# Causal mask and row maxima of the second attention: product on TensorE and reduction, or one fused pass on VectorE

## The reference

```python
def _L1_attn_ref(x, W_qkv, W_o):          # x: 8 x 256 x 128, 16 heads of 8 features
    q, k, v = split(x @ W_qkv)
    q, k = _rope(q, k)
    att = einsum('bhtd,bhsd->bhts', q, k) / sqrt(8)
    att = att + triu(full((256, 256), -inf), 1)
    w = softmax(att, axis=-1)
    y = einsum('bhts,bhsd->bhtd', w, v)
    return concat_heads(y) @ W_o
```

## Time and profile before

| | us |
|---|---|
| runs: median (lowest to highest) of 3 | 635.62 (633.32 to 635.85) |
| the profiled execution's own time | 635.56 |
| its span, first to last instruction | 633.7 |
| TensorE busy | 576.3 (91%) |
| VectorE busy | 404.8 (64%) |
| ScalarE busy | 266.4 (42%) |
| GpSimd busy | 226.7 (36%) |
| mean granted TensorE clock | 0.955 of full speed |

### The profile page before, as it was taken

How to read it: one execution, slowest core, us unless ns; L and a number is a source line. 1 busy time by engine, 2 the same in 40 slices (tenths; PEclk the granted TensorE clock), 3 DMA queues, 4 the chain that set the end, 5 groups by cost and what they waited for, 6 DMA issues and landing times.

```text
span 633.7 us, 11896 instructions
## 1 busy us (share of the span) xinstructions
PE 576.3 (91%) x4428; PEld 447.1 (71%) x4428; DVE 404.8 (64%) x1057; ACT 266.4 (42%) x531; POOL 226.7 (36%) x327
## 2 busy tenths in 40 slices
PE   3899999999987799999789999999889999999994
PEld 3657667766756599899556666665558888888883
DVE  2477877787764733554657788877246666666655
ACT  3586755575630322220055555555632222222220
POOL 2264545554320535363735555554510000000000
PEclk9699999999978999999959999999869999999999
DMA  5953131223000600002221221220000000000000
GB/s 208 324 197 122 69 134 67 102 100 125 10 1 0 252 1 1 1 2 68 70 74 49 63 63 48 68 73 4 4 1 0 2 1 18 1 18 2 1 18 17
DMA packets 25352, 37.64 MB, mean 59 GB/s; under 512 B 3536, under 2 KB 15568, under 8 KB 24912
## 3 DMA queue, kind: packets, MB, share of 16 engines
q1 hardware_dynamic: 25296, 36.89, 17.5%
HBM read 10.01 MB, written 1.05 MB: 17 GB/s over the span
## 4 chain that ended last, share of the span: by engine, by line
PE 63%; DVE 18%; issue 8%; ACT 3%; POOL 3%; DMA 2%; SPq 2%; POOLq 0%; DVEq 0%; ACTq 0%
PE f_O L1611 7%; PE f_O L801 6%; PE f_H L59 5%; PE f_H L61 5%; PE f_H L60 5%; PE a_MI L485 5%; DVE a_UA L366 4%; PE a_S L1328 4%; PE a_Y L437 4%; PE a_YP L1357 3%; PE a_S L1336 3%; PE a_PJ L59 2%; DVE a_m L1172 2%; PE a_S L423 2%; DVE a_rr L357 2%
## 5 line engine op out<-in xcount | busy, mean ns | idle before, releaser
L226 POOL TENSOR_TENSOR a_Y<-a_Y 128x256 f32<-128x256 f32 x64 | 59.5, 933 | 97.0 <-ACT a_Y L265 97.0
L366 DVE SCALAR_TENSOR_TENSOR a_UA<-a_UA,a_mask 128x768 f32<-128x768 f32 x64 | 68.3, 1075 | 27.1 <-ACT a_UA L273 26.6
L1172 DVE TENSOR_REDUCE a_m<-a_S 128x3 f32<-128x384 f32 x117 | 63.7, 554 | 31.6 <-PE a_S L1336 26.5
L1479 ACT ACTIVATE f_sg<-f_H 128x512 f32<-128x512 f32 x64 | 38.2, 597 | 103.1 <-PE f_H L61 103.1
L1557 DVE TENSOR_TENSOR f_hid<-f_H,f_sg 128x512 f32<-128x512 f32 x64 | 44.3, 692 | 53.2 <-PE f_H L61 43.1
L273 ACT ACTIVATE a_UA<-a_S,a_one 128x768 f32<-128x768 f32 x64 | 57.6, 900 | 44.8 <-PE a_S L424 44.6
L1096 POOL TENSOR_SCALAR_AFFINE_SELECT f_w<-f_w 128x256 f32<-128x256 f32 x128 | 51.8, 407 | 67.9 <-ACT f_w L1143 67.7
L1143 ACT ACTIVATE f_w<-a_ST 128x384 f32<-128x384 f32 x118 | 56.9, 493 | 39.7 <-PE a_ST L1334 39.7
L1611 PEld LDWEIGHTS f_O<-f_w,f_hid 128*128 128x128 f32 x512 | 65.9, 191 | 8.1 <-issue 3.3
L1611 PE MATMUL f_O<-f_w,f_hid 128*128 128x128 f32 x512 | 67.8, 276 | 2.0 <-DVE f_acc L1535 2.0
L437 PE MATMUL a_Y<-a_UA,a_V 128*64 128x256 f32 (+1 forms) x512 | 58.4, 351 | 0.0
(11 more groups left out here) (282 smaller groups left out, 1390.0 us busy)
## 6 DMA issues: line engine op xcount, KB each, us to landing
a_q<-a_c_h SPq DMA_DIRECT2D x16, 256.0 KB, 2.5
a_q<-a_c_l SPq DMA_DIRECT2D x16, 256.0 KB, 2.6
a_k<-a_c_h SPq DMA_DIRECT2D x16, 256.0 KB, 2.5
a_k<-a_c_l SPq DMA_DIRECT2D x16, 256.0 KB, 2.6
f_w<-in_f_w SPq DMA_DIRECT2D x1, 2048.0 KB, 8.8
a_q<-a_c_h SPq DMA_DIRECT2D x16, 128.0 KB
a_q<-a_c_l SPq DMA_DIRECT2D x16, 128.0 KB
a_k<-a_c_h SPq DMA_DIRECT2D x16, 128.0 KB
```

The source lines that it names most:

```text
L226: pool.tensor_tensor(Y2[:, v % 2, j, :], Y[:, v % 2, j, :], Y[:, v % 2, j, :], ALU.mult).then_inc(y2_ready, 1)
L366: dve.scalar_tensor_tensor(UA[:, j % 4, :, :], UA[:, j % 4, :, :], 1.0, mask[:, None, :].to_broadcast([P, 2, SW]), ALU.add, ALU.mult).then ...
L1172: dve.tensor_reduce(m3[:, b % 2, h % H1, :], s_bank(h)[:, 0:SW].rearrange("p (a n) -> p a n", a=3), AX.X, ALU.max).then_inc(max_done, 1)
```

## The change

The mask product is gone from both places, and the S products are each complete by themselves (`stop=True`). `s_ready` is now raised by the second S product. On VectorE each head has two fused passes in place of the reduction: one over the 256 columns of the second half of the queries, one over the 128 of the first. Each adds the mask to the scores, writes the sum as bf16 to `masked` (four buffers, which nothing reads) and writes the maximum over its columns to one column of `row_max`. `mask_b` keeps its size, but its first 128 columns are now zeros: the pass over 256 columns reads all of it, the pass over 128 its second half. `row_max` has the layout that mm had, so L1176, L1177 and `mm_ready` go, and in place of the wait for `mm_ready` a batch waits for `mx_ready` of the batch two before it.

```diff
-        m3 = sb("m3", [P, 2, H1, 3])
-        mm = sb("mm", [P, 2, H1])
+        row_max = sb("row_max", [P, 2, 2, H1])
+        masked = sb("masked", [P, 4, SW], BF16)
...
                     if b >= 2 and h % H1 == 0:
-                        dve.wait_ge(mm_ready, 2 * (b - 1))
-                    dve.tensor_reduce(m3[:, b % 2, h % H1, :], s_bank(h)[:, 0:SW].rearrange("p (a n) -> p a n", a=3), AX.X, ALU.max).then_inc(max_done, 1)
+                        dve.wait_ge(mx_ready, b - 1)
+                    for t, cols in ((1, slice(0, L)), (0, slice(L, SW))):
+                        width = P + t * P
+                        i = dve.tensor_tensor_reduce(out=masked[:, h % 4, cols], in0=s_bank(h)[:, cols], in1=mem["mask_b"][:, L - width:L], scale=1.0, scalar=-3e38,
+                                                     op0=ALU.add, op1=ALU.max, accum_out=row_max[:, b % 2, t, h % H1:h % H1 + 1])
+                    i.then_inc(max_done, 1)
                 if maxima_at(g, MAX - 2) is not None:
                     b = maxima_at(g, MAX - 2)
                     dve.wait_ge(max_done, (b + 1) * H1)
-                    dve.tensor_tensor(mm[:, 1, :], m3[:, b % 2, :, 0], m3[:, b % 2, :, 1], ALU.max).then_inc(mm_ready, 1)
-                    dve.tensor_copy(mm[:, 0, :], m3[:, b % 2, :, 2]).then_inc(mm_ready, 1)
-                    dve.wait_ge(mm_ready, 2 * b + 2)
...
-                    by_pair = mm[:, :, :].rearrange("p t (j r) -> p t r j", r=2)
+                    by_pair = row_max[:, b % 2, :, :].rearrange("p t (j r) -> p t r j", r=2)
...
-                for n in heads:
-                    pe.matmul(s_bank(n)[:, P:SW], mem["ident_b"][:, :], mem["mask_b"][:, :], start=False, stop=True, skip_group_check=True).then_inc(s_ready, 1)
...
-                    pe.matmul(S[h % 2][:, L:SW], sq[:, 0:P], sk[:, 0:P], start=False, stop=False, skip_group_check=True)
+                    pe.matmul(S[h % 2][:, L:SW], sq[:, 0:P], sk[:, 0:P], start=True, stop=True).then_inc(s_ready, 1)
...
-                    pe.matmul(S[h % 2][:, P:SW], mem["ident_b"][:, :], mem["mask_b"][:, :], start=False, stop=True, skip_group_check=True).then_inc(s_ready, 1)
...
-    a["mask_b"] = f(np.tile(np.where(n > m, -3e38, 0.0), (1, 2)).astype(bf16))
+    a["mask_b"] = f(np.concatenate([np.zeros((P, P)), np.where(n > m, -3e38, 0.0)], 1).astype(bf16))
```

More of the change, by code:

```diff
@@ L992, in attention1 @@
         s_ready, max_done = sem("s_ready"), sem("max_done")
-        mm_ready = sem("mm_ready")
         mxh_ready, mx_ready = sem("mxh_ready"), sem("mx_ready")
@@ L1268, in score_pair @@
                     sq, sk = operands(n)
-                    pe.matmul(s_bank(n)[:, 0:L], sq[:, P:L], sk[:, 0:L], start=True, stop=False, skip_group_check=True)
+                    pe.matmul(s_bank(n)[:, 0:L], sq[:, P:L], sk[:, 0:L], start=True, stop=True)
                 for n in heads:
                     sq, sk = operands(n)
-                    pe.matmul(s_bank(n)[:, L:SW], sq[:, 0:P], sk[:, 0:P], start=False, stop=False, skip_group_check=True)
-                for n in heads:
-                    pe.matmul(s_bank(n)[:, P:SW], mem["ident_b"][:, :], mem["mask_b"][:, :], start=False, stop=True, skip_group_check=True).then_inc(s_ready, 1)
+                    pe.matmul(s_bank(n)[:, L:SW], sq[:, 0:P], sk[:, 0:P], start=True, stop=True).then_inc(s_ready, 1)
                 for _ in range(10 if h < 4 else 2):
@@ L1327, in _ @@
                 if h is not None:
-                    pe.matmul(S[h % 2][:, 0:L], sq[:, P:L], sk[:, 0:L], start=True, stop=False, skip_group_check=True)
+                    pe.matmul(S[h % 2][:, 0:L], sq[:, P:L], sk[:, 0:L], start=True, stop=True)
                 if head_at(g) is not None:
```

## The result

The changed kernel takes 639.04 us (median of 20 runs, 634.82 to 647.24), the kernel before 633.12 us (20 runs, 632.35 to 637.76). The ratio is 1.0087, with a 95% interval of 1.0068 to 1.0106: slower by 0.9%. The forecast was no change, 635.7 us from a base of 635.6. The profiled execution took 638.9 us with a span of 637.1; that of the kernel before took 635.56 us with a span of 633.7. The medians hold every execution; the ratios leave out those more than 1.5% above the fastest of their kernel.

The account below looks back on a forecast made before the run. VectorE was to become the bound by 4 us per batch, where neither engine alone had been. From 635.6 us, -1.7 at half clock and +1.8 over the full-clock batches gave 635.7 us, range 628 to 652.

Parts of the forecast that it names:

- What bounds the kernel now: Second attention, per batch of 16 heads: neither engine alone; VectorE 15.0 us and TensorE 15.6 us of work in 18.1.
- What TensorE sheds: Mask product gone: 0.13 us saved per head at full clock, 2.1 us per batch, leaving TensorE 13.5 us.
- What VectorE takes on: Two fused passes and two read-outs replace one reduction of 0.46 us per head; new price 0.67 us.
- T: VectorE's price per head for two fused passes and their read-outs: 0.67 us, break-even at 0.65.
- Rivals 2 and 3: Fused passes: read-out waits for its pass, 0.83 us per head, 650 us, chance 0.12; nothing overlaps, 1.01, 670 us, chance 0.10.
- L1176 and L1177: Two small VectorE instructions per batch go, saving 0.81 us; the split reading the maxima directly adds nothing.
- the 6.8: VectorE's other work per batch, in us, after taking out 16 reductions at 0.46 and the two small instructions.
- Sum per batch: Full-clock batch: VectorE 17.5 us plus 0.9 of waits, 18.4 against 18.1; +1.8 us over 6.1 batches.
- Rival 1: Full-clock batches: TensorE was the bound, VectorE's waits nearly vanish; 17.3 us per batch, 628 us in all, chance 0.10.
- The first stretch: First seven heads, at half clock from 324.28 to 334.32 us, TensorE alone the bound: 1.7 us saved.
- Rival 4: Granted clock falls in the middle of the stage because TensorE idles more: 645 us, chance 0.08.
- After 441 us no maxima are left: Stage's end: nothing changes there; the gain of the last two removed small instructions is counted at nothing.

Follow-up runs that it names:

- the start's dummies: Changed kernel with eight dummy products in place of two behind each pair of scores of heads 16 to 22: 637.24 us, ratio 1.0065.

## Why the prediction failed, point by point

**The step that failed** is the granted clock: the sum took it as unchanged, and counted the part after 441 us at nothing. It fell, and the stage's end took 8.0 us more. The sum per batch was off too, the other way: +0.3 us forecast and -1.2 measured. The measured 639.0 us lies within the stated 628 to 652, and even within the forecast's own 630 to 642, by luck: the two errors partly cancel, and that spread was meant for VectorE's price and waits, not for the clock.

**What bounds the kernel now**: right that neither engine alone does. TensorE's own work fell from 15.6 to 12.9 us (16.9 less 4.0 of waits), and VectorE's is 15.6. So VectorE leads by 2.7 us and not by 4, and the batch became shorter by only 1.2 of the 2.7 us that TensorE shed; the rest went into its waits for VectorE, 4.0 us where it was 2.5. The 4 us rested on mis-sized terms.

**What TensorE sheds**: I took 0.13 us per head, near the lower end. In the chain it is 0.21 to 0.22, the upper one: a group now holds it for 0.38 us (428.80 to the next piece, a value product, at 429.18) where it was 0.60. The product held the chain for all of its piece, and nothing of it came back as the next group's weights. By a batch's sum, 15.6 - 12.9, it is 0.17. In a batch TensorE's busy time fell to 14.0 us:

```profile
353.70:370.60 16.90, 13.99 (x163) 10.10 (x163) 15.25 (x94) 10.32 (x28) 9.87 (x21) 1.00 0.26 69
```

**What VectorE takes on**: T is 0.56 us, not 0.67. The timeline of two passes and their read-outs, to be held against the earlier trace rows:

```profile
374.33 0.42 DVE L1173 CUSTOM_DVE_ANT_0 a_masked<-a_S,mask_b 128x256 bf16<-128x256 f32 x1
374.68 0.08 DVE L1173 DVE_READ_ACCUMULATOR2_ANT a_row_max<- 128x1 f32 x1
374.68 0.28 DVE L1173 CUSTOM_DVE_ANT_0 a_masked<-a_S,mask_b 128x128 bf16<-128x128 f32 x1
374.89 0.08 DVE L1173 DVE_READ_ACCUMULATOR2_ANT a_row_max<- 128x1 f32 x1
374.89 0.42 DVE L1173 CUSTOM_DVE_ANT_0 a_masked<-a_S,mask_b 128x256 bf16<-128x256 f32 x1
```

The passes are 0.35 and 0.21 (I had 0.33 and 0.20). Each read-out is recorded at the same time as the next pass and adds nothing, where I took 0.07 from the pairs in the earlier trace rows. By the rule of the Trainium skill, "VectorE: DVE Perf Modes", section "The DRAIN you can't avoid", the next operation would have to wait for the pipeline; the same section adds that one which is not held starts earlier. The starts above, 0.35 apart at a duration of 0.42, are of the second kind. Rivals 2 and 3, which needed 0.83 and 1.01 us per head, are refuted.

**L1176 and L1177**: their 0.81 us are gone, but a part comes back in the split behind them, which lasted 0.25 us before:

```profile
387.76 0.77 DVE L1183 CAST a_mx<-a_row_max 128x16 fp32r<-128x16 f32 x2
```

The prediction had the split add nothing; some 0.5 of the 0.8 us moved into it. By the prediction's own sum VectorE's work per batch would be 6.8 + 0.5 + 16 x 0.56 = 16.3 us; it is 16.9 less 1.3 of waits, 15.6. The 0.7 between is a third error, in the 6.8: seven reductions of a batch stood ahead of a wait, where each costs its 0.555 and not the 0.46 to the next start, 7 x 0.095 = 0.7. From 389.1 to 406.0 us VectorE waits 1.3 us for TensorE, of which I had said some 1 us, and TensorE waits 4.0 for it, well over 2.5, as I had said too:

```profile
PEld a_S L1326 <- DVE a_row_max L1173: 2.7, 4, 1.5
PE a_S L1326 <- DVE a_row_max L1173: 1.3, 1, 1.3
DVE a_masked L1173 <- PE a_S L1330: 1.3, 3, 0.6
```

**Sum per batch**: forecast 18.4, measured 16.9 where the clock holds. So the middle of the stage should have brought -1.2 x 6.1 = -7 us and not +1.8; the kernel without the product and with the reduction, whose clock held until 429 us, went from the first mark to the last in 95.9 us against 102.9, 7.0 less. The kernel before was not as even as the prediction took it: its batches took 16.91, 18.08, 18.10, 18.11, 16.84 and 14.84 us. Rival 1 was the nearer one for this part by its 17.3 us, but not by its mechanism, which had VectorE's waits vanish.

**The first stretch**: I had -1.7 us for its first seven heads. They took 8.9 us (324.12 to 332.97) in place of 10.0 (324.28 to 334.26), 1.1 less, since at half clock groups start 0.95 us apart where it was 1.16, 0.21 less and not 0.24, and some heads have other work between them. The first mark is 1.7 us early all the same; that the figure comes out is in part luck.

At an unchanged clock the kernel would have come to 635.6 - 1.7 - 7.0, about 627 us, by this estimate. The kernel with 32 products and the start's dummies reaches 627.7, but by other terms: its last two batches take 16.84 and 14.66 us, as in the kernel before, a fall near 344 us makes its second batch 18.08 us, and it gains 3.0 in the end, where the kernel before had a fall of its own.

**Rival 4 is what happened.** I gave it 0.08, put it in the middle of the stage and priced it at 645 us. The mechanism was right, a falling clock behind a TensorE with less to do, and its row too: the earlier trace rows already showed a fall with TensorE busy for 1.38 of 2 us. Two things were wrong. The chance was too low, since I set against it that the stretches in between are busier; but the three falls came right behind light stretches, and the lightest went from 1.09 to 0.50 of 2 us. And the place: two short dips in the middle (the first cost about 1.5 us, one batch taking 18.41 where its neighbours took 16.93), and 8.0 us in the end, where **"After 441 us no maxima are left"** is the sentence that failed. No instruction changed there, but the clock that it inherits did.

The spread of the 20 runs points the same way. The shortest, 634.82 us, had a mean clock of 0.934; 638.9 had 0.925, 642.7 had 0.918, and the longest, 647.24, had 0.903. It is no straight line: one of 638.8 us had 0.918 too.

**What is shown and what is argued.** Shown: leaving out the product shortens a batch by 1.1 to 1.3 us, with or without fused passes; the clock has fallen by 433 us in all three traced kernels without it or any addition to the batch, and stays low for 44 us in two of them; putting 32 of 105 such products back removes, in the traced execution, the long low stretch and 11 us of the end. Argued only: that it is the light stretch behind VectorE's norm that lets the clock fall. For it speaks that between 336 and 450 us the clock falls 24 times in the fourteen traces, each time close behind 2 us in which TensorE was busy for only 0.33 to 1.05, and that the kernel before, with and without dummies, has neither such a stretch (its lightest are 1.09 and 1.08) nor a fall there. Against it as the sole cause stands that many light stretches pass without a fall. In the kernel with a dummy in front of each head two of 0.9 did; and at 362 us in the changed kernel, and in the kernel without the product and with the reduction at 412 us, TensorE was as idle as ahead of the falls and the clock stayed:

```profile
412.00:414.00 2.00, 0.52 (x10) 0.36 (x7) 1.90 (x8) 1.15 (x3) 1.08 (x2) 1.00 0.54 141
```

Not tried: the norm spread over several heads, or a third score bank, so that TensorE would not wait there.

## What to carry to other kernels

When a change takes work from TensorE, read the granted clock beside what it did just ahead of each fall, not its mean share alone, and follow the clock into the stages behind, where nothing was edited. A removed product can free the whole piece that it holds in the chain (0.21 us here), but the loop gives back only what the other engine lets through: 1.2 us per batch of 16 heads here, 0.07 per head. A small read-out behind a pass may be free (0.00 here). If a removal gains per batch and loses at the end, keep the removed work for the part just before the end: that gave both gains here, 627.7 to 629.0 us against 633.4, though not in every execution.

## What the runs showed of the hardware

- The granted clock stayed at 0.50 (1.2 GHz) for 44 us, although TensorE was busy for 9.5 of 10 us:

```profile
440.00:450.00 10.00, 9.54 (x62) 5.98 (x60) 2.49 (x12) 4.54 (x12) 3.23 (x8) 0.50 0.01 3
```

  In the traced execution of the kernel with dummies in the end it stayed so at 19.81 of 20 us. The Trainium skill, "TensorE: Matmul & The Clock Gate", Part 1, has activity release the lower level; these rows do not show that, while the short dips agree with it (from 382 to 384 us TensorE was busy for 2.00 of 2, and the clock was back at 1.00 by 386). Why it stays low in the end is open; with the start's dummies alone it came back for 6 us at 450, behind 17.35 us of work in 18.
- A product over the whole array in front of a group cost more (18.5 us per batch) than the same one behind it (18.0), with fused passes in both.
- Four dummies together behind a transpose cost 1.5 us per batch of 16 heads more than none (18.4 against 16.9).
- Among the small instructions that read the maxima one takes some 0.6 to 0.8 us, and not always the first: L1176 before (0.69), L1183 after (0.77), but L1183 (0.66) and not L1176 (0.17) in the kernel without the product and with the reduction. What makes it long is open.
